# A 512-column add in place of four fused multiply-adds: every second expert's output goes through ScalarE

## The reference, cut to what matters

```
def _L1_ffn_ref(x, gate_w, gate_b, W1, b1, W2, b2):       # xf: 16384 x 128
    probs = softmax(xf @ gate_w + gate_b)
    top2_vals, top2_idx = top_k(probs, 2)
    cw = zeros((N, 8)).at[rows, top2_idx].add(top2_vals)  # zero for the other six
    def step(acc, params):                                # once for each expert
        w1, bb1, w2, bb2, we = params
        h = gelu(xf @ w1 + bb1)
        y = h @ w2 + bb2
        return (acc + we[:, None] * y, None)
```

## Time and profile before

| | |
|---|---|
| median of three runs | 3469.91 us |
| the profiled execution | 3460.26 us |
| its span, first to last instruction | 3458.5 us |
| granted TensorE clock, mean | 0.85 |
| PE busy | 2574.0 us, 74% |
| DVE busy | 2453.2 us, 71% |
| ACT busy | 1765.3 us, 51% |
| POOL busy | 1156.7 us, 33% |

### The profile page before, as it was taken

The page is one execution under the profiler, slowest core; times in us unless marked ns, Lnnn a source line. Parts: engine busy times, 40 slices in busy tenths (PEclk is TensorE's granted clock), DMA queues, the critical chain, the costliest instruction groups (busy, mean ns, idle before and its releaser), DMA issues.

```text
span 3458.5 us, 48939 instructions
## 1 busy us (share of the span) xinstructions
PE 2574.0 (74%) x15405; PEld 1900.7 (55%) x15406; DVE 2453.2 (71%) x7195; ACT 1765.3 (51%) x3180; POOL 1156.7 (33%) x1205
## 2 busy tenths in 40 slices
PE   1788888888888851212888878788787888888899
PEld 0566666666666631112565656556565566566666
DVE  6788778877778754435677768677876777686774
ACT  0566656666666510112555455555555555555654
POOL 0000000000000005765565665656565655555200
PEclk7899999999999965555788988989888888888899
DMA  2011111111111013222333323232333233233300
GB/s 89 31 49 43 49 43 49 47 46 38 42 49 37 31 65 97 44 58 63 84 67 81 73 64 91 62 91 65 84 69 84 68 75 82 61 87 69 81 13 10
DMA packets 228556, 210.48 MB, mean 61 GB/s; under 512 B 70781, under 2 KB 160585, under 8 KB 227657
## 3 DMA queue, kind: packets, MB, share of 16 engines
q1 hardware_dynamic: 190008, 190.83, 18.6%
q0 software_dynamic: 37280, 14.38, 5.1%
q10 hardware_dynamic: 1008, 2.15, 0.2%
HBM read 159.49 MB, written 47.74 MB: 60 GB/s over the span
## 4 chain that ended last, share of the span: by engine, by line
DVE 26%; PE 15%; another core or an unknown queue 9%; issue 9%; ACT 1%; DVEq 1%; SPq 0%; DMA 0%; ACTq 0%
DVE keep_x L2190 7%; PE lay_b_y L1804 6%; PE lay_b_z L1795 5%; DVE lay_oht L2095 1%; DVE lay_hid L2116 1%; DVE lay_oh L2092 1%; PE lay_b_b L1846 1%; DVE lay_split L1079 1%; DVE lay_stats L2215 1%; DVE lay_split L1080 1%; DVE lay_split L1076 1%; PE lay_b_att L1771 1%; PE lay_b_g L1896 1%; DVE lay_look L1073 1%
## 5 line engine op out<-in xcount | busy, mean ns | idle before, releaser
L1757 POOL DMA_INDIRECT lay_got<-node_table,lay_idx x1152 | 1132.1, 983 | 761.9 <-issue 308.6
L1804 PEld LDWEIGHTS lay_b_y<-lay_w,lay_hid 128*128 128x128 f32 x4096 | 535.7, 205 | 154.9 <-issue 152.9
L1795 PE MATMUL lay_b_z<-lay_xin,lay_w 128*128 128x512 f32 x1024 | 577.2, 692 | 11.4 <-ACT lay_hid L1949 8.3
L1804 PE MATMUL lay_b_y<-lay_w,lay_hid 128*128 128x128 f32 x4096 | 546.7, 288 | 29.9 <-issue 27.3
L2190 DVE SCALAR_TENSOR_TENSOR keep_x<-lay_b_y,lay_gates,keep_x 128x128 f32<-128x128 f32 x1024 | 287.5, 343 | 376.7 <-remote 211.3
L1949 ACT ACTIVATE lay_hid<-lay_b_z,lay_b 128x512 f32<-128x512 f32 x512 | 328.8, 682 | 395.0 <-PE lay_b_z L1795 199.9
L885 POOL MEMSET find_no_src<- 128x9 int32 x1 | 0.1, 107 | 1239.8 <-POOLq L48 1239.8
L2037 ACT ACTIVATE lay_unused<-lay_hub_wide,lay_halves 128x1152 bf16<-128x1152 uint16 x256 | 320.3, 1251 | 133.7 <-DMA lay_hub_wide<-sorted_dst 111.3
L468 PE MATMUL front_b_h<-front_xt,front_m 128*128 128x512 f32 x512 | 272.8, 664 | 59.5 <-ACT front_act_m L578 30.9
L1795 PEld LDWEIGHTS lay_b_z<-lay_xin,lay_w 128*128 128x128 f32 x1024 | 201.0, 218 | 175.3 <-issue 153.1
L224 DVE TENSOR_TENSOR sort_keys<-sort_keys 128x1024 f32<-128x1024 f32 (+2 forms) x182 | 257.4, 1414 | 42.4 <-ACT sort_keys L546 39.9
(11 more groups left out here) (398 smaller groups left out, 4249.7 us busy)
## 6 DMA issues: line engine op xcount, KB each, us to landing
lay_wide<-sorted_dst SPq DMA_DIRECT2D x128, 288.0 KB
lay_hub_wide<-sorted_dst SPq DMA_DIRECT2D x128, 288.0 KB
made<-front_y SPq DMA_DIRECT2D x128, 256.0 KB, 2.0
lay_y<-made SPq DMA_DIRECT2D x32, 1024.0 KB
lay_got<-node_table,lay_idx POOLq DMA_INDIRECT x1152
front_adj<-in_adj SPq DMA_DIRECT2D x32, 256.0 KB, 3.0
keep_x<-in_x SPq DMA_DIRECT2D x32, 256.0 KB, 3.4
lay_adj<-in_adj SPq DMA_DIRECT2D x32, 256.0 KB
```

The lines of the kernel that those rows point to most:

```text
L1757: pool.indirect_dma_start(out=got[:, b % RING, c, :], out_offset=None, in_=table, in_offset=bass.IndirectOffsetOnAxis(ap=idx[:, b % AHEAD, ...
L1795: pe.matmul(b_z[c][:, :], w1[:, e, P * c:P * c + P], flat(xin[g % 2][:, :, :]), start=True, stop=True).then_inc(z_done, 1)
L1804: mm = pe.matmul(b_y[n % 2][:, P * j:P * j + P], hid[n % 2][:, c, P * j:P * j + P], w2[:, e * HK + c, :], start=(c == 0), stop=(c == HK - 1))
```

## The change

Experts with an odd number leave their bank in another way. ACT gets a function `weigh(g, e)`, called behind the gelu in `expert(g, e)` when e is odd. It waits for the gates and for `y_done`, and does four activations of 128 columns (Copy, with the gate as the scale for each partition) from `b_y` into a new tile `weighed`, of which there are two. The last adds one to the new semaphore `y_weighed`. DVE's `expert(1, f, e)` with odd e waits for `y_weighed` in place of `y_done`, and adds the whole tile to x with one `tensor_tensor` of 512 columns. `down` of an odd expert waits for `y_weighed` of the odd expert before it, in place of `y_added`. Even experts stay as they were.

The diff also merges twelve semaphores of an earlier program, `find_blocks`, into two, `v_step` and `pe_step`, with the same waits by other counts. Of that a part is shown.

```diff
-        diag_ready = s.sem("diag_ready")
-        below_ready = s.sem("below_ready")
-        rows_summed = s.sem("rows_summed")
-        row_ready = s.sem("row_ready")
+        v_step = s.sem("v_step")
+        pe_step = s.sem("pe_step")
...
-            pe.wait_ge(row_ready, 1)
+            pe.wait_ge(v_step, 2)
...
+        weighed = [s.sb(f"weighed{k}", [P, TB, P]) for k in range(2)]
...
+        y_weighed = s.sem("y_weighed")
...
             def down(g, e):
                 n = g * E1 + e
                 pe.wait_ge(hid_ready, HK * n + HK)
-                after(pe, y_added[1], n - 1)
+                if n % 2:
+                    after(pe, y_weighed, n // 2)
+                else:
+                    after(pe, y_added[1], n - 1)
...
                 if n + 1 < groups * E1:
                     gelu(n + 1)
+                if e % 2:
+                    weigh(g, e)
+
+            def weigh(g, e):
+                n = g * E1 + e
+                act.wait_ge(gates_ready[1], g + 1)
+                act.wait_ge(y_done, n + 1)
+                after(act, y_added[1], n - 3)
+                for j in range(TB):
+                    ins = act.activation(weighed[n // 2 % 2][:, j, :], b_y[n % 2][:, P * j:P * j + P], ACT.Copy,
+                                         scale=gates[1][:, g * TB + j, e:e + 1])
+                ins.then_inc(y_weighed, 1)
...
-                else:
+                elif e % 2 == 0:
                     v.wait_ge(y_done, u + 1)
                     made_here = b_y[u % 2][:, :]
                 if e > 0:
                     v.wait_ge(y_added[n], u)
+                if n == 1 and e % 2:
+                    v.wait_ge(y_weighed, u // 2 + 1)
+                    v.tensor_tensor(x[:, of(g), :], x[:, of(g), :], weighed[u // 2 % 2][:, :, :], ALU.add)\
+                        .then_inc(y_added[1], 1)
+                    return
                 for j in range(TB):
```

More of the change, by code:

```diff
@@ L916, in _ @@
             pe.wait_ge(consts, 16)
-            pe.wait_ge(below_ready, 1)
+            pe.wait_ge(v_step, 1)
             pe.matmul(banks[0][:, 0:2 * blocks], ones[:, :], below[:, :], start=True, stop=True)
@@ L931, in _ @@
                               start=True, stop=True).then_inc(rows_out, 1)
[L933 removed]
+            pe.wait_ge(v_step, 3)
             pe.matmul(banks[0][:, 0:1], shift_up[:, :], begin[:, 0:1], start=True, stop=False)
@@ L937, in _ @@
             pe.matmul(banks[0][:, 1:2], sum_to_last[:, :], valid[:, :], start=False, stop=True)\
-                .then_inc(end_done, 1)
+                .then_inc(pe_step, 1)
             pe.wait_ge(rest_ready, 2)
-            pe.matmul(banks[0][:, 2:3], ones[:, :], any_rest[:, :], start=True, stop=True).then_inc(end_done, 1)
-            pe.wait_ge(diag_ready, 1)
+            pe.matmul(banks[0][:, 2:3], ones[:, :], any_rest[:, :], start=True, stop=True).then_inc(pe_step, 1)
+            pe.wait_ge(v_step, 4)
             pe.matmul(banks[3][:, 0:2 * blocks], ones[:, :], begin_diag[:, :, :].rearrange("p u b -> p (u b)"),
-                      start=True, stop=True).then_inc(end_done, 1)
-            pe.wait_ge(n_ready, 1)
+                      start=True, stop=True).then_inc(pe_step, 1)
+            pe.wait_ge(v_step, 5)
             pe.matmul(banks[1][:, 0:2], upto[:, :], n_win[:, :], start=True, stop=True)
-            pe.matmul(banks[2][:, 0:2], ones[:, :], n_win[:, :], start=True, stop=True).then_inc(n_summed, 1)
+            pe.matmul(banks[2][:, 0:2], ones[:, :], n_win[:, :], start=True, stop=True).then_inc(pe_step, 1)
             for u in range(2):
-                pe.wait_ge(inside_ready, u + 1)
+                pe.wait_ge(v_step, u + 6)
                 pe.matmul(banks[4 + 2 * u][:, 0:gmax], ones[:, :], offset[:, u, :], start=True, stop=True)
                 pe.matmul(banks[5 + 2 * u][:, 0:gmax], block_no[:, :], inside[:, u, :], start=True, stop=True)\
-                    .then_inc(tables_done, 1)
+                    .then_inc(pe_step, 1)
         @block.vector
@@ L987, in _ @@
             v.tensor_scalar(any_rest[:, :], rest_low[:, :], drop_key, None, ALU.is_lt).then_inc(rest_ready, 1)
-            v.wait_ge(rows_summed, 1)
+            v.wait_ge(pe_step, 1)
             v.tensor_scalar(row_of[:, :], banks[0][:, 0:2 * blocks], iota_p[:, 0:1], None, ALU.is_equal)\
-                .then_inc(row_ready, 1)
+                .then_inc(v_step, 1)
             me.mark(v.tensor_copy(before_n[:, :], banks[1][:, 0:2]))
@@ L1003, in _ @@
                                            op0=ALU.mult, op1=ALU.add))
-            v.tensor_scalar(begin[:, :], begin[:, :], float(n_edges), None, ALU.min).then_inc(begin_ready, 1)
-            v.wait_ge(begin_ready, 1)
+            v.tensor_scalar(begin[:, :], begin[:, :], float(n_edges), None, ALU.min).then_inc(v_step, 1)
+            v.wait_ge(v_step, 3)
             whole_stretches(v, me, begin, begin_at)
@@ L1013, in _ @@
                     me.mark(ins)
-            ins.then_inc(diag_ready, 1)
-            v.wait_ge(end_done, 2)
+            ins.then_inc(v_step, 1)
+            v.wait_ge(pe_step, 3)
             me.link(v.tensor_scalar(any_rest[:, :], banks[0][:, 2:3], 1.0, float(cols), ALU.min, ALU.mult))
@@ L1026, in _ @@
                     me.mark(ins)
-            ins.then_inc(n_ready, 1)
-            v.wait_ge(end_done, 3)
+            ins.then_inc(v_step, 1)
+            v.wait_ge(pe_step, 4)
             me.mark(v.memset(tables["first"][:, :, blocks:], n_edges))
@@ L1031, in _ @@
                                   banks[3][:, 0:2 * blocks].rearrange("p (u b) -> p u b", u=2)))
-            v.wait_ge(n_summed, 1)
+            v.wait_ge(pe_step, 5)
             me.mark(v.tensor_copy(upto_n[:, :], banks[1][:, 0:2]))
```

14 lines of the change are left out of this document (4 added, 10 removed).

## The result

The changed kernel took 3610.62 us, the median of four runs (3598.19 to 3614.94). Four runs of the kernel before took 3470.18 us (3456.33 to 3479.88). The ratio is 1.040, with a 95% interval of 1.037 to 1.043: slower by 4.0%. The profiled execution took 3598.19 us, 137.9 us more than the one before. The forecast was 3593 us with a range of 3530 to 3635, and for the profiled execution 3590.

What follows compares the result with a forecast made beforehand. No engine is full; a loop of waits through expert 7, DVE's work to `xn2` and PE's second part sets the step. 119 us for 27 steps plus the rest, together 130, gave 3593 us (3590 for the profiled execution), range 3530 to 3635.

Steps and rivals of the forecast that it cites:

- The loop of waits: Last program's steps: expert 7's result, 24.7 us of DVE work to `xn2`, then 35.6 us to the next expert 7.
- expert 7's place in it: ACT's `weigh` of expert 7 queues behind `keep_att`, table load and gelu, so DVE's bias starts 3.9 us later (3.6 to 4.3).
- The price of the four activations: ACT's four 128-column activations in `weigh`: 1.25 us, with bounds of 0.9 and 1.64 us.
- The sign "1.2 to 1.3 us": In the changed kernel's timeline, ACT's four activations should take 1.2 to 1.3 us.
- The other three odd experts: Experts 1, 3 and 5 by ACT: only expert 5 lengthens a step, by 0.5 us, bounds 0 and 1.0.
- expert 1: nothing; expert 3 covered; expert 5: 0.5: Expert 1 costs nothing, expert 3's late `normalise` has 0.9 us of cover, expert 5's late `h` costs 0.5 us a step.
- The sum: 27 steps with edge blocks x (3.9 + 0.5) = 119 us, with the rest 130 us; bounds 103 and 155 us.
- The steps without edge blocks and the last expert: End of the last program: 10 us for three starts (4 + 4 + 2), and 0.9 us for the very last expert 7.
- The signs: Changed timeline: bias 5.2 us after `keep_att`, DVE's idle ahead of expert 7 up 4 to 5 us, step 64 to 65.
- The lag absorbs it: Late use of PE's results takes up DVE's delay: half absorbed 3525 us, fully 3462; chances 0.12 partly, 0.05 fully.
- DVE is the bound: DVE's own work sets the step, so 1.8 us less over 32 steps gives 3403 us; chance 0.08.
- ACT's delays run on: Activations take 1.64 us, `normalise` loses its cover, expert 5 counts in full: step grows 7 us, 3660 us; chance 0.07.

Runs made afterwards that it cites:

- only7: The changed kernel with only expert 7 leaving its bank by ACT, experts 1, 3 and 5 by DVE as before: 3583.33 us, ratio 1.034 to the kernel before.
- wait_alone: No `weigh`; against the kernel before, DVE's add of expert 7 only also waits for ACT's gelu of the next group's first expert: 3559.77 us, ratio 1.027.
- not7: The changed kernel with experts 1, 3 and 5 by ACT and expert 7 by DVE as before: 3483.69 us, ratio 1.006 to the kernel before.
- one_three: The changed kernel with only experts 1 and 3 by ACT, 5 and 7 by DVE, on a second chip: 3210.59 us, ratio 1.006 to the kernel before.
- first23: Second mixture as in the kernel before; ACT scales the first mixture's experts 2 and 3 in place, DVE adds 512 columns each: 3155.80 us, ratio 0.990.
- before_again: The kernel before, unchanged, run once more with a profile on a third chip: 3195.1 us, step 51.86 us.

## Why the prediction was right

**The loop of waits, and expert 7's place in it.** The prediction put `weigh` of expert 7 behind `keep_att`, a table load and a gelu, and the bias 5.2 us after `keep_att` and 3.9 us later than before. It is 5.13 us, 3.8 later. The first block and `xn2` moved by 3.9 and 4.0. `only7` gives 3.99 us a step for this term, and `wait_alone` shows that 3.49 of it is the queue's order and no work.

**The price of the four activations.** Taken as 1.25 us, measured as 1.14 for four in a row, 371 ns for one by the mean; the 1.64 us of the normalisation stayed a matter of its form. The Trainium skill, "ScalarE: Activation LUTs", "What ACT_TABLE_LOAD costs", made 1.27 us of it and "VectorE: DVE Perf Modes", in the trn2 errata, 1.0; the measured value lies between the two. The sign "1.2 to 1.3 us" was a little too long.

**The other three odd experts.** The step "expert 1: nothing; expert 3 covered; expert 5: 0.5" came out with about the right sum, in the wrong place, and that is luck. `not7` gives 0.72 us where 0.5 was taken, with bounds of 0 and 1.0, but `one_three` shows as much without expert 5. For expert 1 no cost of its own shows. For expert 3 the prediction asked only whether `normalise` stays covered, and it does. It left out DVE's own wait for `weigh` of expert 3, which the mean over the steps puts at 3.60 us in the changed kernel against 1.58 before. It also had no term for the clock.

**The sum.** 27 steps by 4.4 made 119 us; 27 steps by 4.60 were 124.3. Of the bounds, the lower one was added to the profiled execution and the upper one to the median; from the profiled execution the upper bound is 3615 us, still above the 3598 measured. The steps without edge blocks and the last expert made 10.9 by the forecast, and 9.5 + 2.9 = 12.4 in the trace. The start, 1.2 us, was not counted. Together 138 for 130 us, and most of the miss is the 0.2 us a step.

**The signs.** DVE's idle time ahead of expert 7 was to grow by 4 to 5 us. In the step shown it grew by 3.1, and in the mean by 5.1 (4.5 before, 9.7 after). The step was to be 64 to 65 us and is 63.8 by the mean; the 60.3 us that the prediction started from was one of the longer steps, the mean being 59.2. ACT's late `weigh` of expert 3 brought another wait of DVE, 4.06 us at 2653.48 against 1.28 in the earlier trace rows. In the table the last 0.45 us arise between `turn_att` and `keep_att` (3.65 us before, 4.10 after), after the part where the prediction looked for them. In `only7` that stretch is 3.32 us and `turn_att` 4.32 later. How a step's length is shared between PE's records and this lag varies from kernel to kernel.

**The rivals.** *The lag absorbs it* falls by the step of 63.8 us. It falls more clearly on the chip where the lag is 0.67 us in place of 3.65: the change costs 1.041 there and 1.040 here. *DVE is the bound* was half right and is the useful half. It does set the pace up to `xn2`, and `first23` gains 1%, about two thirds of it by taking 0.88 us from it there; the adds that the change takes from it lie elsewhere. The errata rule for operations of 512 elements, from "VectorE: DVE Perf Modes" in the Trainium skill, agrees with the trace on the operation (692 ns against 1.13 us for the four) and says nothing of where it stands. The page gives it for operations that read SBUF, and the four that the change replaced read a bank as well. *ACT's delays run on* did not come: the step grew by 4.6 us and not by 7.

## What to carry to other kernels

An operation that is handed to another engine joins that engine's queue, so price its place and what stands ahead of and behind it before its duration: here 3.5 of 4.0 us a step came with no work at all. Taking work from an engine helps only in the stretch where others wait for it; the same trade of four operations for one cost 3.4% at expert 7 and, done twice, gave 1% where DVE had no idle time and ACT had some. A bank that two engines pass on can be worth more freed early than drained cheaply, as expert 0 showed. Read waits and offsets as means over many steps: a single step gave 60.3 us for a step of 59.2, and 3.1 us for a wait that grew by 5.1.

## What the runs showed of the hardware that was not expected

**The same kernel takes 3462 us on one chip and 3189 to 3190 on two others.** The difference lies in one part of the program. From 0 to 1200 us the busy times agree; from 2500 to 2700 PE and DVE do more in the same time on the second kind. Windows of the kernel before in `before_again`:
```profile
0.00:1200.00 1200.00, 959.14 (x5617) 710.35 (x5619) 939.21 (x1856) 692.74 (x1331) 0.84 (x7) 0.95 0.14 46
2500.00:2700.00 200.00, 174.82 (x1155) 132.46 (x1154) 171.51 (x616) 127.78 (x219) 134.36 (x141) 0.93 0.40 89
```
and the first of them in the profile shown ahead of the prediction:
```profile
0.00:1200.00 1200.00, 958.95 (x5649) 711.60 (x5650) 938.80 (x1856) 696.72 (x1339) 0.83 (x7) 0.94 0.14 46
```
What differs is when others use PE's results. `turn_att` and then ACT's `keep_att` in `before_again`:
```profile
2474.32 0.60 PE L1872 MATMUL lay_b_g<-lay_ident,lay_att 128*128 128x128 f32 x4
```
```profile
2474.96 0.60 ACT L1972 ACTIVATE lay_att_t<-lay_b_g 128x512 f32<-128x512 f32 x1 [2.45 <-PE lay_b_g L1872]
```
That is 0.64 us from start to start. In the profile ahead of the prediction it is 4.34 us, from 2658.65 in the earlier trace rows to this:
```profile
2662.99 0.60 ACT L1972 ACTIVATE lay_att_t<-lay_b_g 128x512 f32<-128x512 f32 x1 [4.27 <-remote]
```
On that chip DVE's waits for `down` appear as "remote", with no releaser that the profile can name, for 131.5 us between 2000 and 3000 us; in `before_again` none does, and PE is named. The median of a matmul's duration is the same, 275 ns on both, but not the time at the lower clock: PE spends 16.7 us of a step at 1.2 GHz on the first chip and 8.1 in `before_again`. The matmuls of `apply_att` (L1880), which stand behind the wait for `keep_att`, take 429 ns by the mean from 2000 to 3000 us against 303. The same on both is the last step without edge blocks: 41.35 us in `before_again`, by the starts of `keep_att` at 3084.12 and 3125.47, against 41.3 ahead of the prediction. The late results therefore go with the stretch where the edge blocks and their gathers run. What holds them back is open, and no run here was made to find it. How much of the longer step is the lag and how much the clock is open too. A forecast from a profile of such a chip has to take the lag as it is. It hardly changed the ratio of this change, 1.040 with the lag and 1.041 without.
